# Transposes of the probabilities right behind the mask product, in eleven of sixteen slots

## What is computed

```
x = layernorm(x + up(expert[dom](gelu(down(x)))))             # front: adapter with a chosen expert
x1 = layernorm(x) * (1 + scale) + shift                       # conditioned by a timestep
q, k, v = x1 @ Wq, x1 @ Wk, x1 @ Wv                           # 16 heads of 16 columns
p = softmax(q k^T / 4 + side[head], masked)                   # per head 256 x 256
x2 = x1 + (p v) @ Wo ; x3 = x2 + gelu2(ln(x2) @ W1) @ W2      # feed-forward, 1024 wide
x4 = x3 + MLP of one of three kinds(x3) ; f = layernorm(x4)
out = relu(f + dt * (first and second differences of grids * f))
```

## Time and profile before

| | |
|---|---|
| median of 3 runs | 883.87 us (882.42 to 885.88) |
| the profiled execution, its own time | 884.87 us |
| its span, first to last instruction | 883.1 us |
| PE busy | 816.8 us (92%), 5968 products |
| PE weight loads busy | 698.2 us (79%) |
| DVE busy | 737.9 us (84%) |
| ACT busy | 621.9 us (70%) |
| POOL busy | 163.7 us (19%) |
| mean granted TensorE clock | 0.960 |
| chain that ended last | PE 85%, DVE 9%, issue 2%, ACT 1%, DMA 1% |

### The profile page before, as it was taken

The page is one execution under the profiler, slowest core; times in us unless marked ns, Lnnn a source line. Parts: engine busy times, 40 slices in busy tenths (PEclk is TensorE's granted clock), DMA queues, the critical chain, the costliest instruction groups (busy, mean ns, idle before and its releaser), DMA issues.

```text
span 883.1 us, 18591 instructions
## 1 busy us (share of the span) xinstructions
PE 816.8 (92%) x5968; PEld 698.2 (79%) x5968; DVE 737.9 (84%) x2474; ACT 621.9 (70%) x1284; POOL 163.7 (19%) x160
## 2 busy tenths in 40 slices
PE   5568999999999999999999999999999999998791
PEld 2447678888888898888888888888888888787581
DVE  5664777898989899898989898998989898969555
ACT  2244767887878787878778787878787887777230
POOL 3010102222122203031211222030302112201200
PEclk9667999999999999999999999999999999999996
DMA  5942879576776756576766767595857576591110
GB/s 176 276 125 85 171 184 203 139 175 162 161 184 168 196 137 170 152 195 155 174 162 169 185 156 192 138 187 147 186 158 174 157 166 166 139 203 43 54 36 12
DMA packets 147593, 137.33 MB, mean 156 GB/s; under 512 B 19282, under 2 KB 144787, under 8 KB 147492
## 3 DMA queue, kind: packets, MB, share of 16 engines
q1 hardware_dynamic: 147172, 135.80, 61.9%
q10 hardware_dynamic: 320, 0.26, 0.1%
HBM read 98.23 MB, written 4.23 MB: 116 GB/s over the span
## 4 chain that ended last, share of the span: by engine, by line
PE 85%; DVE 9%; issue 2%; ACT 1%; DMA 1%; POOL 0%; SPq 0%; POOLq 0%; DVEq 0%
PE back_bank L1115 13%; PE turn_bank L1071 12%; PE context_bank L1125 7%; PE score_bank L1192 7%; PE score_bank L1193 6%; PE front_bank L1109 5%; PE back_bank L1109 5%; PE attend_bank L1109 5%; PE front_bank L1142 4%; PE back_bank L1095 3%; PE front_bank L1298 3%; PE back_bank L1086 3%; PE attend_bank L1095 3%; PE attend_bank L1056 2%; PE front_bank L1346 2%
## 5 line engine op out<-in xcount | busy, mean ns | idle before, releaser
L549 ACT ACTIVATE sc<-sc,negmax 128x256 f32<-128x256 f32 x512 | 231.2, 504 | 21.9 <-DVE negmax L911 21.4
L911 DVE CUSTOM_DVE_ANT_0 sc<-score_bank,side 128x256 f32<-128x256 f32 x512 | 195.5, 420 | 37.0 <-PE score_bank L1193 33.0
L526 ACT ACTIVATE pt<-turn_bank 128x512 f32<-128x512 f32 x176 | 105.9, 602 | 133.9 <-PE turn_bank L1071 112.8
L1071 PE MATMUL turn_bank<-ident,sc 128*128 128x128 f32 x1024 | 157.9, 277 | 1.1 <-ACT sc L549 1.0
L1071 PEld LDWEIGHTS turn_bank<-ident,sc 128*128 128x128 f32 x1024 | 123.8, 142 | 31.9 <-issue 13.7
L1192 PE MATMUL score_bank<-ks,qs 128*128 128x256 f32 x512 | 124.1, 324 | 7.2 <-DVE negmax L911 6.7
L1115 PE MATMUL back_bank<-w,ffT 128*128 128x256 f32 x512 | 118.0, 379 | 0.0
L1115 PEld LDWEIGHTS back_bank<-w,ffT 128*128 128x128 f32 x512 | 97.0, 190 | 12.7
L1193 PE MATMUL score_bank<-mask_neg,ident_r 128*128 128x512 f32 x256 | 103.1, 403 | 0.0
L466 POOL TENSOR_TENSOR rstd<-var,half_neg 128x2 f32<-128x2 f32 x64 | 49.9, 780 | 272.6 <-DVE var L836 271.0
L1192 PEld LDWEIGHTS score_bank<-ks,qs 128*128 128x128 f32 x512 | 79.4, 195 | 16.1 <-DVE negmax L911 9.1
(11 more groups left out here) (217 smaller groups left out, 1975.4 us busy)
## 6 DMA issues: line engine op xcount, KB each, us to landing
side<-in_side SPq DMA_DIRECT2D x128, 512.0 KB, 5.4
qs<-qh SPq DMA_DIRECT2D x128, 64.0 KB, 4.3
qs<-ql SPq DMA_DIRECT2D x128, 64.0 KB, 4.1
ks<-kl SPq DMA_DIRECT2D x128, 64.0 KB, 4.3
wb<-in_wb SPq DMA_DIRECT2D x16, 512.0 KB, 7.1
ks<-kh SPq DMA_DIRECT2D x124, 64.0 KB, 3.8
xN<-in_x SPq DMA_DIRECT2D x16, 256.0 KB, 5.0
wc<-in_wc SPq DMA_DIRECT2D x16, 256.0 KB, 3.0
```

Of the source, the lines that this page charges most:

```text
L526: e.activation(pt[:, h % NP2, :, :], two(tbank[h % 2]), ACT.Copy).then_inc(copied[h % 4], 1)
L549: i = e.activation(sc[:, h % NS, q, :], sc[:, h % NS, q, :], ACT.Exp, bias=negmax[:, q, h:h + 1], scale=-1.0)
L911: i = e.tensor_tensor_reduce(sc[:, s % NS, q, :], two(sbank[s % 2])[:, q, :], side[:, (H * X.i + s) % NSIDE, q, :], -1.0, 3.4e38, ALU.add, ...
L1071: i = e.transpose(tbank[h % 2][:, k * S + q * P:k * S + q * P + P], sc[:, h % NS, q, k * P:k * P + P], ident[:, :])
```

## The change

Only PE's order of instructions changes. The four transposes of head s-2 (`four(flip)`, or the loop `for n in range(4): flip(n)`, which do the same) move up so that they stand right behind the mask product and ahead of the slot's other products, in slots 0, 1, 6, 7, 8, 14 and 15 wholly; in the other four they move ahead of only a part of these: in slot 3 behind the transposes of x3 and ahead of `differ`, in 10 behind the mix and n3's transposes and ahead of the adapter's product, in 12 and 13 behind the W1 quarter and ahead of the adapter's product. In slots 6 and 14 the order of the rest is turned round too: the mix now stands ahead of the block of twelve products (q in slot 6, the fourth W1 quarter in slot 14). Slots 2, 4, 5, 9 and 11 stay. No wait, semaphore or buffer is added or removed.

```
                     if s == 0 and T:
+                        four(flip)
                         quarter(e, "ff_ready", T, 2)
                         second_ff(T, ((1, 0), (1, 1), (1, 2), (1, 3), (0, 4), (0, 5)), no_more)
+                    elif s == 1 and T:
                         four(flip)
-                    elif s == 1 and T:
                         quarter(e, "ff_ready", T, 3)
                         second_ff(T, ((0, 6), (0, 7), (1, 4), (1, 5), (1, 6), (1, 7)), no_more).then_inc(ev["w2_done"], 1)
-                        four(flip)
...
                             turn(bbank, x3, ev["x3_turned"])
+                        four(flip)
                         if U:
                             differ(U, 1)
-                            four(flip)
-                        else:
-                            for n in range(4):
-                                flip(n)
...
                     elif s == 6:
-                        if F:
-                            e.wait_ge(ev["x1T_ready"], times(F, 2))
-                            project_T_parts(fbank, wq, wql, 0, x1h, x1l, KT, ev["q_done"])
+                        for n in range(4):
+                            flip(n)
                         if X:
                             e.wait_ge(ev["v_ready"], X.n)
                             wait(e, ev["ct_hi"], X.p)
                             mix(X, 0)
-                        for n in range(4):
-                            flip(n)
+                        if F:
+                            e.wait_ge(ev["x1T_ready"], times(F, 2))
+                            project_T_parts(fbank, wq, wql, 0, x1h, x1l, KT, ev["q_done"])
                     elif s == 7:
+                        four(flip)
                         if B:
                             e.wait_ge(ev["ctxn_hi"], B.n)
                             turn(abank, ctxN, ev["c2_turned"])
                         if T:
                             e.wait_ge(ev["gb_ready"], T.n)
                             project(bbank, gbT, wc, ev["c_done"], no_more)
-                            four(flip)
-                        else:
-                            for n in range(4):
-                                flip(n)
...
                     elif s == 8:
+                        four(flip)
                         if B:
                             e.wait_ge(ev["ctxT_ready"], B.n)
                             project(abank, ctxT, wo, ev["wo_done"], no_more)
-                            four(flip)
-                        else:
-                            for n in range(4):
-                                flip(n)
...
                             turn(abank, n3, ev["n3_turned"])
+                        for n in range(4):
+                            flip(n)
                         if G:
...
                             i.then_inc(ev["down_done"], 1)
-                        for n in range(4):
-                            flip(n)
...
                             project_T_parts(abank, w1, w1l, 2 * P, n3h, n3l, 2, ev["w1_done"])
+                        for n in range(4):
+                            flip(n)
                         if G:
...
-                        for n in range(4):
-                            flip(n)
                     elif s == 13:
...
                             project_T_parts(bbank, w1, w1l, 4 * P, n3h, n3l, 2, ev["w1_done"])
+                        for n in range(4):
+                            flip(n)
                         if G:
...
                             i.then_inc(ev["up_done"], 1)
+                    elif s == 14:
                         for n in range(4):
                             flip(n)
-                    elif s == 14:
+                        if X:
+                            e.wait_ge(ev["ct_lo"], X.n)
+                            mix(X, 2)
                         if B:
                             quarter(e, "u1_ready", B, 1)
                             project_T_parts(abank, w1, w1l, 6 * P, n3h, n3l, 2, ev["w1_done"])
-                        if X:
-                            e.wait_ge(ev["ct_lo"], X.n)
-                            mix(X, 2)
-                        for n in range(4):
-                            flip(n)
                     elif s == 15:
+                        four(flip)
                         if B:
                             quarter(e, "u1_ready", B, 2)
                             quarter(e, "ff_ready", B, 1)
                             second_ff(B, ((0, 0), (0, 1), (0, 2), (0, 3)), no_more)
-                            four(flip)
-                        else:
-                            for n in range(4):
-                                flip(n)
```

## The result

The changed kernel took 910.90 us in the median of 4 runs (906.30 to 912.37) against 884.27 us (882.42 to 885.88): a ratio of 1.0293, 95% interval 1.0249 to 1.0337, slower by 2.9%. The forecast was 904.3 with a range of 891 to 914.

What follows compares the result with a forecast made beforehand. PE, busy for the whole 48.38 us steady turn, was taken as the bound. 1.1 us per turn over 14 turns (15.5), plus start 2.0 and end 2.9, gave 20.4, a median of 904.3, forecast as 904 (891 to 914).

Steps and rivals of the forecast that it cites:

- What bounds the kernel: Steady turn: PE is busy for all 48.38 us, so only a shorter PE list wins; each new wait is lost.
- New neighbours: Slots 6 and 14: twelve products behind a mix cost 0.08 us per turn; eight places behind float32 blocks cost nothing.
- First wait: Slot 14: PE's moved mix waits for ACT's copy of head 11, about 0.65 us per turn (0.5 to 0.75).
- Second wait: Next turn's slot 0: late w1_done delays head 14's exp; PE's transposes wait 0.3 us (0 to 0.45).
- The other slots: Slots 6 and 7 hold narrowly; later wo_done in slot 8 costs 0.08 us; DVE passes on little of slot 3's d_done.
- The start: Turn 0, slot 6: query products now stand behind a mix and its copy, 2.0 us once (0 to 2.1).
- The end: Last turn: 1.4 us through head 5's exp, 1.6 for twelve products, 0.3 for head 14, minus 0.4; together 2.9.
- The forecast case: Both waits come: time between 898 and 911 us, chance 0.68.
- One wait only: Rival: ACT catches up, so the second wait and the end extras vanish; about 895 us, chance 0.12.
- exposed loads: Rival: weight loads lie open in eight places behind float32 blocks, 0.19 us each; 915 us, chance 0.08.
- no change: Rival: the moved work is as well hidden as before; 884 us, chance 0.06.
- faster: Rival: no wait in slots 14 or 0, as ACT copies head 11 at least 0.65 us sooner; 879 us, chance 0.06.

Runs made afterwards that it cites:

- act_only: Kernel before, PE's order old; only ACT's order edited: head 11's copy ahead of the third eviction, r2_h and head 12's copy ahead of the fourth; 884.28 us.
- eight: Kernel before with the new order in slots 0, 1, 7, 8, 10, 12, 13 and 15 only; slots 3, 6, 14 old; 888.43 us.
- undo3: Changed kernel with slot 3 in its old order, `differ` ahead of the transposes; 908.15 us.
- only14: Kernel before with slot 14 alone in the new order; 894.32 us.
- undo7: Changed kernel with slot 7 in its old order, transposes behind `project(bbank, gbT, wc)`; 905.48 us.
- copy11: Changed kernel, PE untouched; in slot 13 ACT copies head 11 ahead of the third W1 quarter's eviction instead of behind it; 896.76 us.
- undo14: Changed kernel with slot 14 in its old order; 890.95 us.
- mix14late: Changed kernel, but in slot 14 only the transposes stand early; the mix stays behind the twelve W1 products; 889.67 us.
- undo0: Changed kernel with slot 0 in its old order, transposes of head 14 behind W2; 904.33 us.

## Why the prediction was right, point by point

**What bounds the kernel.** Shown for this kernel: every wait put into a turn in which PE has no pause is in the turn's length (49.71), and an earlier copy by ACT where PE does not wait for it (act_only) changes nothing.

**New neighbours.** The 0.08 for slots 6 and 14 together measured 0.12, some 0.06 in each. The eight places behind float32 blocks were taken at nothing and measured nothing (eight, at 48.37). The rule of the Trainium skill ("TensorE: Matmul & The Clock Gate", section "The mechanism") that was weighed there would have made this turn about 49.9, by an estimate from 48.37 and eight times the 0.19 of a load; the run does not agree with it.

**First wait.** Forecast at 0.65, with 0.5 to 0.75 around it; measured 0.72. The missing part is the handover: the mix starts 0.15 after the copy's end, while the transposes start 0.05 after the exp's.

**Second wait.** Forecast at 0.3; the transposes lost 0.31 and the slot 0.35. ACT's idle time ahead of the fourth `ffT` was forecast at about 1.5 and is 1.54. The turn, 49.71, lies just above the 49.3 to 49.6 that the prediction named as its sign.

**The other slots.** Slots 6 and 7 held, as forecast. The 0.08 for the later wo_done was an overestimate (slot 10: 0.03). One term was costed at next to nothing and was not: the later d_done in slot 3, of which "DVE passes on little", passed through t_e, a bias and the lower heads' context into 0.11 of slot 5 (undo3).

**The sum.** Forecast 1.1 us per turn, measured 1.34. Over 14 turns that is 18.8 instead of 15.5.

**The start** was taken at 2.0, a figure that no run confirms or excludes. In turn 0 the late queries do show, as slot 7 takes 3.4 instead of 2.3, but the first mask product of turn 1 follows that of turn 0 after 50.7 us in the changed kernel and 51.2 before. The two are not alike in their clock: the setup block of the last section takes 3.6 us in the one and 4.7 in the other. The distance is 48.6 to 51.2 in the three profiles with PE's old order up to slot 13 (before, only14, act_only) and 48.9 to 54.7 in the ten others, so the spread is larger than the term.

**The end** was 4.1 instead of 2.9. Its chain:

```profile
807.54 0.92 ACT sc L549 x2
808.50 0.66 PE turn_bank L1071 x4
809.15 0.44 PE attend_bank L1056 x4
809.59 1.74 PE back_bank L1095 x8
811.36 0.76 DVE x L965
...
830.03 0.99 PE context_bank L1125 x16
831.02 1.63 PE attend_bank L1109 x12
...
834.92 0.92 ACT sc L549 x2
835.88 0.66 PE turn_bank L1071 x4
```

The exp of head 5, the transposes, then the products and DVE's x4 stand one behind the other as forecast, 1.0 in slot 7 instead of 1.4 (undo7). The twelve products behind the mix are there too: slot 14 of that turn takes 5.4 instead of 4.0. The undersized term is the second wait: the exp of head 14 is on the chain with 0.92, and from the last mask product to the last mix it takes 10.3 us instead of 9.5, where the forecast had the two small terms cancel. Two parts had no term for this turn: 0.35 in its slot 0 and 0.4 in its slot 10 (4.5 instead of 4.1). The latter comes with the order of eight too (4.5); its cause was not looked for.

**The total.** 18.8 + 4.1 = 22.9, and the profiles differ by 904.5 - 883.1 = 21.4. Turns 1 to 14 sum to 19.1 (687.1 against 668.0), the end to 4.1, the time behind the last mix to 0.2, and turn 1 begins 1.9 earlier (101.0 against 103.0). The medians differ by 26.6 in the first measurement and by 23.7 in the second. The first is 5 us above what the profiles show; no term of the forecast stands for these 5 us, and their cause is open. The forecast case reached to 911, so 910.90 lies at its edge and 906.97 well inside.

**The rivals.** One wait only, exposed loads, no change and faster are each excluded by a turn length: 49.71 with both waits in it, 48.37 for the eight places. The faster rival's turning point, a copy of head 11 that ends 0.65 us earlier, was produced on purpose in copy11: the wait goes, but the gain that the rival put behind it does not come. With both waits gone PE's turn is 48.65, never below 48.37.

**Open.** Eight, undo14 and mix14late are 5 to 8 us over the kernel before, while their turns account for 0 to 3 and their ends for under 2. Where the other 2 to 4 us lie is not shown, because profiles with the same order of PE differ by as much. Turn 4's first mask product comes at 239.4 us in the kernel before and at 237.3 in act_only, and at 240.1, 241.1 and 238.6 in the three. From the last mix to the end of the span eight takes 1.3 us longer than the kernel before, and so does act_only.

## What to carry to other kernels

Here, moving work ahead on the engine that is busy throughout could not win the time for which others waited; it lost the cover under which their lateness lay. Before moving a consumer, compare its new place with the end of what it waits for, and then do the same for whatever the passed-over block releases: here the second wait came from the event of the block that was passed. Ten of eleven moves together cost 0.17 us per turn, even with margins of 0.4 us. The one with its margin below zero cost 0.74 by itself (only14), and it made a second wait at one of the others, slot 0.

## What the runs showed of the hardware

**The clock at which a setup block ran differed between executions.** In turn 0, 32 float32 products of one column (L1176) run once. In two profiles, first of the changed kernel, then of undo3, PE's timeline and the busy time of the stretch in which they run (granted clock third from the right):

```profile
82.58 3.63 PE L1176 MATMUL back_bank<-cols,ffT 128*128 128x1 f32 x32
```

```profile
82.58:86.21 3.63, 3.63 (x35) 3.63 (x34) 0.00 (x0) 0.60 (x1) 0.00 (x0) 1.00 0.20 62
```

```profile
82.06 6.82 PE L1176 MATMUL back_bank<-cols,ffT 128*128 128x1 f32 x32
```

```profile
82.06:88.88 6.82, 6.82 (x34) 6.82 (x33) 0.00 (x0) 0.61 (x1) 0.00 (x0) 0.50 0.06 20
```

The same 32 products took 3.63 us at a granted clock of 1.00 (2.4 GHz) and 6.82 us at 0.50 (1.2 GHz). The clock falls in both, in the first behind the block (0.55 from 86 to 88 us), in the second ahead of it (0.60 from 80 to 82). Before the fall PE was busy for all of 82 to 86 us in the first, and for 0.20 of the 2 us from 78 to 80 in the second. Slot 8 of turn 0 then takes 8.4 or 12.4 us, and turn 1 starts 3.0 us later, counted from turn 0's start. Of the ten profiles with a changed order ahead of slot 14, seven have the block at 3.6 to 3.9 us and three (undo0, undo3, undo7) at 6.8; before, only14 and act_only have it at 4.4 to 4.7. From 100 to 150 us the clock was 1.00 in both.

Both profiles of the changed kernel are of the short kind (3.6 and 3.9), so that this makes its spread from 906 to 912 us is likely but not shown. For it speaks the mean granted clock of the runs: 0.965 in the run of 906.3 us, 0.958 to 0.960 in those of 909.7 to 912.4.

**Weight loads behind a mix lie open, behind a float32 block they don't.** Score pair 0.43 behind a mix and 0.24 behind W2, at the same 128 x 128 weights; the twelve products 1.62 behind a mix and 1.42 otherwise. The mix's products, whose weights are 18 columns wide, follow each other every 0.06 us (0.99 for 16), and the load of the next block takes 0.19. That a load is longer than the distance of the products above it is not the whole reason: the twelve products follow each other every 0.12 us (1.42 for 12), each with a load of 0.19, and nothing lies open there. The reason was not tested.
